# Latent attention: the next batch's value matrices made in the fourth chunk of a batch instead of the third

## The reference, cut to what matters

```python
h0 = rmsnorm(x, ln1_w)                       # per batch of 512 tokens
kv_d, q_d = h0 @ kv_d_w, h0 @ q_d_w          # 512 -> 128 each
k = concat(kv_d @ k_u_w, rope(h0 @ rope_k_w))    # 16 heads of 16 + 16
q = concat(q_d @ q_u_w, rope(q_d @ rope_q_w))
v = kv_d @ v_u_w                             # 128 -> 512: 16 heads of 32
probs = softmax(causal(q @ k.T / sqrt(32)))
h = x + (probs @ v) @ o_w
out = h + moe(rmsnorm(h, ln2_w))
```

## Time and profile before

| | |
|---|---|
| median of the runs | 2498.3 us |
| profiled execution, its own time | 2500.3 us |
| span of that execution's trace | 2498.3 us |
| TensorE busy | 2247.5 us (90%) |
| VectorE busy | 1381.1 us (55%) |
| ScalarE busy | 657.9 us (26%) |
| GpSimd busy | 695.2 us (28%) |
| mean granted TensorE clock | 0.956 of full |

### The profile page before, as it was taken

How to read it: one execution, slowest core, us unless ns; L and a number is a source line. 1 busy time by engine, 2 the same in 40 slices (tenths; PEclk the granted TensorE clock), 3 DMA queues, 4 the chain that set the end, 5 groups by cost and what they waited for, 6 DMA issues and landing times. The chain is left out here.

```text
span 2498.3 us, 29517 instructions
## 1 busy us (share of the span) xinstructions
PE 2247.5 (90%) x10083; PEld 1030.3 (41%) x10086; DVE 1381.1 (55%) x3181; ACT 657.9 (26%) x1163; POOL 695.2 (28%) x1018
## 2 busy tenths in 40 slices
PE   9999997979999999898999997478888888799993
PEld 4444443435444443344444443233333333344441
DVE  6999883436412223555766774955656564422224
ACT  2222321212012121233434333433322322002223
POOL 2210002324523321133433333011113131125553
PEclk9999998999999999998999998689999999999997
DMA  8333102126047776163443330310000000064444
GB/s 293 117 101 112 40 4 72 64 76 243 10 133 247 236 234 202 40 165 83 90 85 78 84 71 2 109 71 1 2 18 2 18 27 18 17 199 83 87 88 149
DMA packets 101697, 235.40 MB, mean 94 GB/s; under 512 B 18919, under 2 KB 42647, under 8 KB 94399
## 3 DMA queue, kind: packets, MB, share of 16 engines
q1 hardware_dynamic: 79006, 191.83, 24.4%
q0 software_dynamic: 22560, 41.87, 7.7%
HBM read 174.69 MB, written 63.53 MB: 95 GB/s over the span
## 5 line engine op out<-in xcount | busy, mean ns | idle before, releaser
L1876 DVE CUSTOM_DVE_ANT_0 D_ps<-D_ps,D_mask 128x256 f32<-128x256 f32 (+1 forms) x512 | 186.9, 420 | 70.7 <-PE D_ps L1773 69.7
L1625 POOL TENSOR_SCALAR_AFFINE_SELECT D_probs<-D_probs 128x256 f32<-128x256 f32 x256 | 106.1, 420 | 286.7 <-ACT D_probs L1683 286.4
L1683 ACT ACTIVATE D_probs<-D_ps 128x512 f32<-128x512 f32 (+1 forms) x256 | 125.3, 543 | 165.0 <-PE D_ps L1795 164.8
L2876 DVE TENSOR_REDUCE F_neg_max<-F_ps 128x4 f32<-128x2048 f32 (+1 forms) x64 | 93.9, 1488 | 107.7 <-PE F_ps L2774 101.6
L3318 PE MATMUL G_ps<-G_gate_up,G_xgT 128*128 x304 | 138.5, 599 | 0.3 <-DVE G_xgT L3409 0.3
L2626 ACT ACTIVATE F_probs<-F_ps 128x1536 f32<-128x1536 f32 (+1 forms) x48 | 76.4, 1591 | 187.2 <-PE F_ps L2790 187.2
L1186 PE MATMUL C_ps<-C_down_shared,C_hs 128*128 128x512 f32 x256 | 114.0, 593 | 3.4 <-DVE C_hs L1353 2.3
L1174 PE MATMUL C_ps<-C_xT,C_gate_shared 128*128 128x512 f32 x256 | 115.4, 593 | 0.6 <-ACT C_xT L1049 0.6
L1174 PE MATMUL C_ps<-C_xT,C_up_shared 128*128 128x512 f32 x256 | 115.1, 592 | 0.0
L1773 PE MATMUL D_ps<-D_k_stack,D_q_stack 96*128 96x256 bf16 (+1 forms) x512 | 93.4, 268 | 8.8 <-DVE D_maxima L1876 7.2
L1023 POOL DMA_INDIRECT expert_sums<-C_y,C_of_slot x32 | 50.2, 1570 | 173.4 <-ACT C_y L1090 108.9
(11 more groups left out here) (496 smaller groups left out, 4531.1 us busy)
## 6 DMA issues: line engine op xcount, KB each, us to landing
C_ring<-moe_experts_dram SPq DMA_DIRECT2D x32, 1536.0 KB, 6.9
qk_parts<-D_parts SPq DMA_DIRECT2D x32, 384.0 KB, 2.5
B_w<-ctx_dram SPq DMA_DIRECT2D x8, 1024.0 KB, 6.0
expert_sums<-A_cq SPq DMA_DIRECT2D x1, 8192.0 KB, 29.4
C_ring<-expert_sums SPq DMA_DIRECT2D x5, 1536.0 KB, 10.4
D_q_stack<-qk_parts SPq DMA_DIRECT2D x16, 384.0 KB, 4.8
D_k_stack<-qk_parts SPq DMA_DIRECT2D x16, 384.0 KB, 7.7
B_w<-ctxT_dram SPq DMA_DIRECT2D x1, 4096.0 KB, 15.9
```

What stands on the lines that cost most here:

```text
L1625: last = nc.gpsimd.affine_select(now[:, :, 0:P], now[:, :, 0:P], [[0, 2], [1, P]], ALU.is_ge, 0.0, base=0, channel_multiplier=-1)
L1683: nc.scalar.activation(probs[at % 2][:, 2 * pair:2 * pair + 2, 0:w], ps[:, 4 + unit % 3, :].rearrange("p (h q) -> p h q", h=2)[:, :, 0:w], ...
L1876: last = nc.vector.tensor_tensor_reduce(now, now, mask[:, first:256], 1.0, -3e38, ALU.add, ALU.max, maxima[n % 2][:, head, t:t + 1])
L2876: last = nc.vector.tensor_reduce(neg_max[n % 2][:, :, t], ps[:, 0:GROUP, at:at + w], AX_X, ALU.max, negate=True)
```

## The change: what it does

Two lines of the planner's input are edited. The four `values` jobs of the next batch leave the list of the third chunk and are put at the end of the list of the fourth. And the fourth chunks no longer have their room set to 1.0 at place 8.

```diff
-        return features(b + 1, 0) + ([("count", b - 1)] if b else []) + values(b + 1) if k == 2 else features(b + 1, 1)[:3]
+        return features(b + 1, 0) + ([("count", b - 1)] if b else []) if k == 2 else features(b + 1, 1)[:3] + values(b + 1)
```

```diff
-            if i == -2 and at == 9 or at == 8 and (i == 0 or i > 0 and i % GROUP > 1):
+            if i == -2 and at == 9 or at == 8 and (i == 0 or i > 0 and i % GROUP == 2):
                 room = 1.0
```

## The result

The changed kernel takes 2503.34 us (median of 20 runs, 2497.3 to 2511.93), the kernel before in the same series 2498.64 us (20 runs, 2490.55 to 2506.54). The ratio is 1.0024, with a 95% interval of 1.0013 to 1.0034: some 5 us slower (4.7 by the medians), which is clear of noise and still inside the half per cent that I called no change. Forecast were 2502.5 us, between 2493 and 2510.

A forecast was written before the change was run, and what follows sets the result against it. TensorE, busy 90% of the span, was taken as the bound. Per batch 0.0 (third chunk) + 0.0 (fourth) + 1.4 us (clock), three times, gave +4.2 us on 2498.3: 2502.5 us, range 2493 to 2510.

The forecast's parts named there:

- The walk through the two chunks: Following the new job order through third and fourth chunks, piece by piece; claimed 0.0 us for each.
- The fourth chunk: Chunks 3, 7, 11: the four moved values are covered by holes of 3.94 us; 0.0 us more.
- The third chunk: Chunks 2, 6, 10: -2.8 then +2.8 us in chunk 2, -1.94 then +1.9 us in the others; 0.0 us.
- the subtraction from chunk 0: Third chunk, slot 4 to slot 5 scores: chunk 0's 9.37 us less 1.38 us gives 8.0 us.
- the length that I named as a sign: Third chunk's expected length as evidence in the profile after: 26.5 + 1.4 = 27.9 us.
- The clock: Behind third-chunk stalls the granted clock drops to 0.50, as in chunk 0: 3 x 1.4 = +4.2 us.
- the new stall: TensorE in chunks 2, 6, 10 waits about 1 us for ScalarE's nope copy, then 2.4 to 3 us for VectorE's join.
- new order in chunk 15: Chunk 15's three pieces keep their TensorE order between the same neighbours; cost 0.
- the first: Rival: clock holds at 1.00 behind the third-chunk stall; 2498.3 us, chance 0.25.
- the second (values uncovered): Rival: fourth chunk doesn't cover the values; 2514.2 us in full, chance 0.07; in part 2505.5 us, chance 0.13.
- the third (features in time): Rival: joins don't hold slot 5, so third chunks lose the whole 3.9 us; 2486.6 us, chance 0.05.
- the fourth (the planner moves less): Rival: the planner moves less than followed, so the change does nothing; 2498.3 us, chance 0.02.

The follow-up runs named there:

- e10: Changed kernel with unread matmuls filling both waits of its third chunks (behind the last nope and for the expert choice): 2493.6 us, ratio 0.9973 to the kernel before.
- e6: Kernel before, values left in third chunks, without room 1.0 at place 8, plus four unread matmuls in each fourth chunk: 2499.0 us, ratio 0.9999.
- e12: Kernel before with two unread matmuls in the wait for the expert choice in chunks 6 and 10: 2500.2 us, ratio 0.9999.
- e11: The changed kernel itself, run once more against the kernel before: 2503.1 us, ratio 1.0013.
- e2: Kernel before with only the room edit (no 1.0 at place 8 of fourth chunks), values not moved: 2497.8 us, ratio 0.9988.
- e3: Changed kernel with the third chunk planned as if the values were still there, features at old places: 2497.0 us, ratio 0.9986 to the kernel before.
- e5: Kernel before with four unread matmuls in each third chunk, behind the values at place 8: 2509.3 us, ratio 1.0042.
- e7: Changed kernel with two values jobs kept in the third chunk, planned as before, and two in the fourth: 2494.4 us, ratio 0.9966 to the kernel before.
- e1: Changed kernel with the room edit taken back (values moved, fourth chunk's room still 1.0 at place 8): 2508.9 us, ratio 1.0039 to the kernel before.
- e4: Changed kernel with unread matmuls behind the last nope (three in chunk 2, two in chunks 6 and 10): 2502.3 us, ratio 1.0003 to the kernel before.
- e9: Two values jobs in each third and fourth chunk, plus two unread matmuls in the expert-choice wait: 2492.5 us, ratio 0.9968 to the kernel before.

## Why the prediction was right, and where it wasn't

The walk through the two chunks held to half a microsecond, and the sign of the clock's term was right. That 4.2 us came so close to the measured 4.7 is in part luck: at the place that I priced, the profile has 1.3 us instead of 4.2, and what made up for it stands at other waits. The reasons follow one by one.

**The fourth chunk: 0.0 us said, 0.14 found.** At full clock it takes 23.14 us (e10) instead of 22.99. The scores of slot 5 come 0.5 us later in the chunk, as said, but by two errors that nearly cancel. I had times_cosine of rope7 behind the middle cut. It belongs to place 4, where GpSimd takes the rotary part first and the cut second, so it stands ahead, and that made the wait of 0.48 us. Against it, the way from turn_m4 to those scores became 1.23 us shorter (3.21 instead of 4.44), where I had 0.97. From the scores to the chunk's end it is 3.86 us instead of 4.21, which is rotate(6) gone from ahead of VectorE's maximum; without the 0.48 us the chunk would by these numbers have ended 0.3 us earlier than before. e6 has the same order, the same wait and the same 0.14 us. The maxima that SyncE stacks later were waited for by nobody, as the walk had it.

**The third chunk: 0.0 us said, -0.4 to -0.5 found.** At full clock 26.56 against 27.04 in chunk 2, 30.39 against 30.77 in chunk 6, 30.60 against 30.97 in chunk 10 (e10 and e12). The stretch with the chain is 7.88 us, where the subtraction from chunk 0 gave 8.0. The earlier part gave 3.15 us in chunk 2 where I had 2.8, and 2.15 us in chunks 6 and 10 where I had 1.94. One number was misread: chunk 2 before begins at 1731.22, not 1731.76, as the row that I took for its first was cut off by my window; it takes 27.04 us, not 26.50. No term of the sum rested on it, but the length that I named as a sign did: 27.9 us for a third chunk, where chunk 2 takes 26.95.

**The clock: +4.2 us said, +3.2 found in the six chunks and about +5 over all runs; the mechanism right, its places and sizes not.** The price behind the new stall was taken from chunk 0, where the whole stretch has the clock at 0.50: 1.4 us. In the profile after, it is 0.61 to 0.64 there, and the stretch takes 0.4 to 0.5 us more than before, 1.3 us in all instead of 4.2; in another run of the same kernel (e11) 1.2 us in chunk 2 and 0.5 us in each of the others. What I left out is that the change also lengthens the wait for the expert choice: I saw that a piece leaves the time ahead of it, and wrote only that the gain is missing. The wait grew by 0.4 us, and the half clock behind it from 2.7 to 2.9 us in chunk 6 and from 1.4 to 2.8 in chunk 10 (the chunk's length less that at full clock, less what lies behind the stall). The other profiles bear this out. Behind this wait at 2.68 to 2.90 us (before, e2, e3, e5, e6 and e7, chunks 6 and 10) the way to the next scores for a maximum takes 5.03 us at full clock; half clock adds 1.25 us to it in the mean, up to 2.8, and nothing in five cases of twelve. Behind it at 3.07 to 3.29 us (the changed kernel twice, e1, e4) the way takes 3.79 us at full clock (e10), and half clock adds 2.8 us in the mean and never less than 1.7.

Summed over the six chunks, from the lengths with and without half clock: before 161.8 us, of which 4.1 us are half clock; after 164.2 us, of which 7.2. So +2.4 us, made of -0.8 for the order and +3.2 for the clock. The profile of e11, the same kernel, has 164.6 us for the six. The other 3.3 us of the 5.6 between the two profiles lie in chunk 9 (+1.6) and from chunk 13 on (+1.6). The change leaves those waits alone; its new order in chunk 15 costs nothing, as said: from that chunk's start to the expert stage it is 73.63 us before, and 73.62 or 73.63 us in e2, e3, e9 and e10, which have that order. The half clock at those places comes and goes (chunk 5 of the changed kernel takes 33.5 us in one run and 31.8 in e11). Outside the six chunks the attention takes 345.4 us (e2) to 352.1 us (e12) in the fourteen profiles, with 346.0 in that of before and 349.3 and 348.5 in the two of the changed kernel. So few profiles can't say if the change makes the half clock there likelier.

The runs as a whole can say more. Over the 101 runs of the kernel before beside the experiments, the mean granted clock is 0.9569, and a run with 0.001 less takes 1.7 us more (a straight line through them). The 20 runs of the changed kernel have 0.9539, or some 15 us more at the lower of the two levels, which by that line is +5.0 us; at the same clock the changed kernel is 0.5 us faster than before, in e11 1.5 us, each with about 1 us of noise. That agrees with -0.8 from the profiles. It takes for granted that the line of one kernel holds for the other. By the same line e3 is 7.9 and e7 6.8 us faster at the same clock, and e5 11.2 us slower, near what was expected of their order alone.

**The rivals.** The clock didn't hold behind the new stall in any of the three chunks, so the first is out; the second (values uncovered) is out by e6; the third (features in time) by the waits at the join; the fourth (the planner moves less) by TensorE's order in the profile, which is that of the table.

The Trainium skill, "TensorE: Matmul & The Clock Gate", section "Loop structure matters more than you think", says that a copy on VectorE doesn't break the engine's warmth; it says so of a loop whose next matmuls follow immediately. My prediction stretched that to stalls of 2.5 to 2.9 us (and called the rival that it bears out the second; it is the first). Behind each of the three stalls, which only ScalarE and VectorE end, the clock is 0.61 to 0.64.

## What to carry to other kernels

Work that is moved away was often somebody's cover: find the wait that it hid, and price that before the gain. Moving as much as the hole takes on one side and as the chain leaves free on the other (two and two here) gave 0.9966, moving all four 1.0024. When a list of jobs is planned by its total, taking jobs out of it also moves those that stay; check where the ones with a deadline land.

## What the runs showed that I had not expected

- The kernel with 13 unread matmuls in TensorE's waits was some 10 us faster (e10 against the changed kernel), with clock 0.960 instead of 0.954 in the mean; the kernel before with four of them was no faster (e12).
- Waits of 1.47 and 2.06 us were followed by 5.3 us at the lower level (e3, chunks 10 and 2), a wait of 2.90 us behind one of 0.79 by a clock of 0.64 in the mean over 4.2 us, and one of 2.89 us by the full clock (e7, chunk 10).
- The place of the half clock wanders from run to run of one kernel, mostly with some 1.6 us a place. Most of the kernel before's spread of 2491.5 to 2509.4 us follows the granted clock (correlation -0.86 over 101 runs).
